# Finer steps, maxima ordered by pairs, a query stack read in halves, and a new order in a three-stage attention kernel

## The chip, the cores and the metric

One core of a Trainium2 chip runs the whole program; the other cores are idle. The time is device microseconds of one execution, and the median of three executions stands for a kernel. The engines are TensorE (PE, with its weight loads PEld), VectorE (DVE), ScalarE (ACT), GpSimd (POOL) and SyncE (SP), which only issues DMAs here.

## The reference

Four batches of x (512 tokens, 128 features) pass three blocks, each on the layer norm of its input, each added to it.

```python
x = x + _L0_attn_ref(_layernorm(x), gamma)          # softmax(-gamma * max(dist_sq, 0)) @ x, 512 x 512
x = x + _L0_xattn_ref(_layernorm(x), ctx, ctx, Wq, bq, Wk, bk, Wv, bv, Wo, bo)
x = x + _L0_ffn_ref(_layernorm(x), router_w, router_b, expert_w, expert_b)
...
dist_sq = sq[:, :, None] + sq[:, None, :] - 2.0 * xy
...
scores = jnp.einsum('bhqd,bhkd->bhqk', q, k) / sqrt(dk)      # 16 heads of 8, 154 keys
scores = scores + slopes[None, :, None, None] * dist[None, None, :, :]
out = einsum('bhqk,bhkd->bhqd', softmax(scores), v)  ... @ Wo.T + bo
...
mask = one_hot(top_k_indices, 8).sum(axis=-2)                # the two best of eight experts
out = einsum('bse,ehd,bsd->bsh', mask, expert_w, hidden_states) + einsum('bse,eh->bsh', mask, expert_b)
```

## The kernel before

The program has five instruction streams. Each is a fixed list of steps, the table `ORDER`: `walk` calls a step `name:b.k` with its batch b and its part k. An engine never leaves its list, so a step that waits on a semaphore holds all that stands behind it. `WARM` says how many matmuls on the constant tile `idle` (results unused) PE issues ahead of a step.

For one batch, with 512 tokens as T = 4 tiles of 128:

- Block 1. `stats1` (DVE) takes mean and variance, `rstd1` (POOL) makes rs and the squared norms `sqp`, `y1` (DVE) normalises. `y1T` (PE, then ACT) transposes y1 and sqp; `dist` makes the four 128x512 distance banks (L913, L914), each reduced on DVE (`rm`, L687) and copied by ACT's relu (L551); `rowmax` and `soft` (L559) make the softmax rows, `probs` transposes them into pT, `self` (L932) multiplies with y1, `gather` (L704, L710, L660, L663) makes x1 and its statistics. There are two distance banks, so tile t waits for the relu of t-2.
- Block 2. `rstd2` makes rs and then x1b = x1 + bo (L521); `y2` (L670), `y2T`, `query` (L945) make q. q is cut into three bf16 parts on ACT and DVE (L757, L759, L761); the last part is there when `q_lo` is counted. SP writes the parts to `q_scratch` and reads them back as `qs`, a stack of 8 head pairs; the key stacks are `kA` (for maxima) and `kB` (for scores). `maxima` (L973, DVE L768) fills a PSUM bank with three query-tile-by-head products of 154 keys and reduces it to negated row maxima `nm`: 64 of them in 22 banks a batch, in two buffers, and two banks are a step. `mcat` cuts nm in three parts, `mT` transposes it, SP carries it through `m_scratch` into six rows of qs. Only then can `scores` (L999 for four banks with the keys over 128, L1003 for sixteen heads; two banks, two items a step) multiply with kB, and ACT's exponential (L611) follows each. `values` (L1019 for the tail keys, L1023) accumulates two halves, `divide` normalises, `aoT` and `wo` (L1050) make x2.
- Block 3. `rstd3`, `y3`, `y3T`, `route` (L1061 and DVE L820 to L835), `mask`, then for each expert `spread` (L1083), `select` (DVE L848) and `experts` (L1096), with `fT` and `store` at the end. Spread uses the banks of the maxima. The last batch does blocks from `divide` on in two halves of 256 tokens.

SP's list holds the DMAs: a load that waits there holds those behind it.

## Time and profile before

| | us |
|---|---|
| median of 3 runs (243.68 to 246.44) | 244.0 |
| the profiled execution | 244.3 |
| its span | 242.5 |
| PE busy, 1206 matmuls | 206.0 (85%) |
| PE weight loads | 104.7 (43%) |
| DVE busy | 157.9 (65%) |
| ACT busy | 109.2 (45%) |
| POOL busy | 36.7 (15%) |
| mean granted clock of PE | 0.972 of full |

The span is cut by the profile into 40 slices, and PE's clock is full in all but two places, at 70 to 80 us and at about 196 us. The chain of work that ended last is PE for 50%, DVE 24%, ACT 9%. In a timeline, neighbouring rows of one engine may overlap a little, since a matmul's row holds its way through the array too: when matmuls follow each other, the distance of their starts is the price of one.

### The profile page before, as it was taken

What the parts mean: (1) busy time and instruction counts of PE and PEld (TensorE: products, weight loads), DVE (VectorE), ACT (ScalarE), POOL (GpSimd) and SP (SyncE); (2) the same over time, 40 slices, a digit from 0 to 9 for tenths busy, and PEclk for the clock granted to TensorE, in tenths of its full rate; (3) what the DMA queues carried; (4) which work ended last, traced back from release to release, by engine and by line L of the source; (5) the groups of instructions that cost most, each with busy time, mean ns of one, the idle gap of its engine ahead of it and who ended that gap; (6) DMA issues with size and microseconds to landing.
All of it is one profiled execution on the core that took longest, in us unless ns stands there. A gap on an engine that the chain in (4) does not pass through costs nothing.

```text
span 242.5 us, 3528 instructions
## 1 busy us (share of the span) xinstructions
PE 206.0 (85%) x1206; PEld 104.7 (43%) x1224; DVE 157.9 (65%) x433; ACT 109.2 (45%) x206; POOL 36.7 (15%) x98
## 2 busy tenths in 40 slices
PE   7488956878958898998999999889987878899994
PEld 2247622436612234474353457643333342335573
DVE  2476536499662488847686699776589513479772
ACT  2286053730317476828635566276133137821300
POOL 5604184300130030005000000130000001002000
PEclk9999999999975999999999999999999979999999
DMA  6997504900204500120152021203601010000011
GB/s 170 310 265 259 110 1 158 223 4 0 57 0 144 119 1 0 41 59 0 68 142 53 0 45 43 58 3 131 130 0 40 11 51 0 0 4 0 1 46 43
DMA packets 23031, 16.91 MB, mean 70 GB/s; under 512 B 10548, under 2 KB 21644, under 8 KB 22924
## 3 DMA queue, kind: packets, MB, share of 16 engines
q1 hardware_dynamic: 23012, 16.67, 26.8%
q8 instruction: 10, 0.16, 0.3%
q14 instruction: 9, 0.07, 0.1%
HBM read 11.29 MB, written 5.37 MB: 69 GB/s over the span
## 4 chain that ended last, share of the span: by engine, by line
PE 50%; DVE 24%; ACT 9%; issue 7%; POOL 4%; DMA 3%; another core or an unknown queue 1%; SPq 0%; ACTq 0%; DVEq 0%; POOLq 0%
DVE nm L768 12%; PE bank L1096 11%; PE bank L875 6%; PE bank L932 5%; PE bank L1023 4%; PE bank L913 4%; PE bank L973 3%; PE bank L1083 3%; DVE y L670 3%; PE bank L1003 3%; POOL rs L459 3%; PE bank L1019 2%; PE bank L870 2%; ACT w L551 2%; DVE x L710 2%
## 5 line engine op out<-in xcount | busy, mean ns | idle before, releaser
L768 DVE TENSOR_REDUCE nm<-bank 128x3 f32<-128x462 f32 x88 | 49.4, 618 | 10.9 <-PE bank L973 10.7
L611 ACT ACTIVATE pt<-bank 128x512 f32<-128x512 f32 x64 | 34.7, 597 | 22.9 <-PE bank L1003 15.2
L973 PE MATMUL bank<-kA,qs 128*128 128x308 bf16 (+1 forms) x172 | 29.2, 264 | 6.5 <-DVE nm L768 5.3
L1096 PE MATMUL bank<-ym,ewT 128*128 128x512 f32 (+1 forms) x80 | 32.5, 511 | 0.3 <-DVE ym L848 0.3
L848 DVE TENSOR_TENSOR ym<-bank,y3T 128x512 f32<-128x512 f32 (+1 forms) x40 | 22.1, 579 | 8.2 <-PE bank L1083 6.8
L870 PE MATMUL bank<-idle 128*128 128x512 bf16 x82 | 22.9, 406 | 3.3 <-DVE idle L655 1.5
L457 POOL TENSOR_SCALAR ve<-mv 128x4 f32<-128x4 f32 (+1 forms) x13 | 2.6, 198 | 151.4 <-DVE mv L663 151.1
L973 PEld LDWEIGHTS bank<-kA,qs 128*128 128x128 bf16 x172 | 12.1, 97 | 28.5 <-DVE nm L768 24.0
L1003 PE MATMUL bank<-qs,kB 128*128 128x512 bf16 x59 | 20.5, 397 | 3.4 <-ACT ptail L611 1.2
L913 PE MATMUL bank<-y1Tg,y1T 128*128 128x512 f32 x32 | 17.9, 641 | 5.5 <-ACT w L551 4.4
L551 ACT ACTIVATE w<-bank,snsq,sgn 128x512 f32<-128x512 f32 x16 | 12.3, 773 | 16.0 <-DVE rm L687 16.0
L687 DVE TENSOR_REDUCE rm<-bank 128x1 f32<-128x512 f32 x16 | 10.9, 688 | 12.6 <-PE bank L914 12.6
L1023 PE MATMUL bank<-pt,vm 128*32 128x512 f32 x128 | 16.9, 598 | 0.3 <-issue 0.3
L670 DVE TENSOR_SCALAR y<-x,mv,rs 128x128 f32<-128x128 f32 x32 | 11.3, 425 | 8.1 <-POOL rs L459 8.0
L1096 PEld LDWEIGHTS bank<-ym,ewT 128*128 128x128 f32 x80 | 13.6, 190 | 5.1 <-DVE ym L848 1.8
L932 PE MATMUL bank<-y,pT 128*128 128x128 f32 x128 | 15.3, 278 | 0.2 <-ACT pT L535 0.2
L870 PEld LDWEIGHTS bank<-idle 128*128 128x128 bf16 x91 | 8.9, 102 | 14.8 <-issue 2.4
L932 PEld LDWEIGHTS bank<-y,pT 128*128 128x128 f32 x128 | 14.6, 192 | 0.6 <-ACT pT L535 0.4
L875 PE MATMUL bank<-ident,y 128*128 128x128 f32 x48 | 7.7, 280 | 6.9 <-DVE y L670 6.9
L559 ACT ACTIVATE w<-w,nrb,sgn 128x512 f32<-128x512 f32 x16 | 12.9, 811 | 1.0 <-DVE nrb L700 0.6
L459 POOL TENSOR_TENSOR rs<-ve,minus_half 128x4 f32<-128x4 f32 (+1 forms) x13 | 13.2, 1012 | 1.1
L1003 PEld LDWEIGHTS bank<-qs,kB 128*128 128x128 bf16 x64 | 6.2, 101 | 14.1 <-ACT pt L611 7.4
(130 smaller groups left out, 275.3 us busy)
## 6 DMA issues: line engine op xcount, KB each, us to landing
qs<-q_scratch SPq DMA_DIRECT2D x8, 384.0 KB, 4.9
q_scratch<-qpart SPq DMA_DIRECT2D x4, 384.0 KB, 2.4
xs<-in_x_dram SPq DMA_DIRECT2D x4, 256.0 KB, 7.2
vm<-in_vm_ones_dram SPq DMA_DIRECT2D x1, 1024.0 KB, 12.0
q_scratch<-qpart SPq DMA_DIRECT2D x4, 256.0 KB, 2.1
kA<-k_scratch SPq DMA_DIRECT2D x8, 120.0 KB, 2.7
kB<-k_scratch SPq DMA_DIRECT2D x8, 120.0 KB, 2.6
out_dram<-ob SPq DMA_DIRECT2D x3, 256.0 KB, 2.4
```

The lines of the kernel that those rows point to most:

```text
L459: g.tensor_tensor(rs[:, at], ve[:, at], minus_half[:, at], ALU.pow).then_inc(rstd[i], 1)
L611: nc.scalar.activation(dst, ST[n % 2][:, :], ACT.Exp).then_inc(exps, 1)
L768: v.tensor_reduce(negated[:, GROUP * g:GROUP * g + heads], MX[n % 2][:, 0:heads * J].rearrange("p (s j) -> p s j", s=heads), AX.X, ALU.max ...
L848: v.tensor_tensor(ym[:, e, at], MX[n % 2][:, at], y3T[:, at], ALU.mult).then_inc(mx_free, 1)
L870: mm(bank_[:, :], idle[:, 0:P], idle[:, :], start=True, stop=True)
L875: last = nc.tensor.transpose(bank_[:, tile(t)], src(t), id_[:, :])
L913: mm((A0S, A1S)[t % 2][b][:, :], y1T[:, tile(t)], y1Tg[:, :], start=True, stop=False)
L932: last = mm(A0S[b][:, tile(t)], pT[:, b % 2, t, u, :], y1[:, b % 2, u, :], start=(u == 0), stop=(u == T - 1))
L973: last = mm(MX[n % 2][:, at * J:(at + heads) * J], qs[:, b % 2, a, tile(t)], kA[:, s:s + heads, a, 0:J], start=True, stop=True)
L1003: last = mm(ST[n % 2][:, :], kB[:, h % 2, h // 2, 0:JM], qs[:, b % 2, h // 2, :], start=True, stop=True)
L1023: last = mm(YV[32 * g:32 * g + 32, :], vm[:, b, R * g + k, :], pt[:, (G * k + g) % PT_RING, :], start=False, stop=(k % 2 == 1), skip_group ...
L1096: last = mm(YMS[b][p][:, at], ewT[:, e, :], ym[:, e, at], start=False, stop=(e == E - 1))
```

## The change

Steps become smaller and the tables that order them are new.

- A scores step is one bank (`PARTS`), a maxima step is one bank (`MAX_GROUPS`), dist is one tile in every batch, self is one tile; `sqT`, `tails` (the products with the tail keys), `invert` (the reciprocal of the softmax sums) and `residual` (x1b) are cut out of larger steps. `residual` has a wait for `q_lo` in front, so x1b is made after the query parts of its batch.
- The maxima run over head pairs first and tiles second: `pieces` and the layout of `nm` change, and the number and width of products in a bank stay.
- The read of qs is four loads in place of two, first pairs 0 to 3, then 4 to 7, with a semaphore each. Maxima wait for the first half at bank 0 and for the second at bank 10.
- `WARM` holds 61 matmuls in place of 91.
- SP has `mT:2` before `store:0`. On POOL, `rstd3:0` comes before `rstd2:2`.

```diff
--- before.py
+++ after.py
@@ ORDER, two of its rows @@
-        y1T:0 dist:0 keys:0 probs:0.0 probs:0.1 probs:0.2 probs:0.3 self:0 y1T:1 y2T:0 query:0 dist:1 probs:1.0
+        y1T:0 sqT:0 dist:0.0 dist:0.1 dist:0.2 dist:0.3 keys:0 probs:0.0 probs:0.1 y1T:1 probs:0.2 sqT:1
...
@@ WARM @@
-    "y1T:0": 14, "probs:0": 1, "y1T:1": 9, "y2T:0": 9, "query:0": 2, "probs:1": 16, "maxima:0": 1, "y2T:1": 16,
-    "query:1": 2, "scores:0": 1, "scores:1": 2, "y2T:2": 3, "wo:1.0": 1, "y3T:1.0": 2, "scores:2": 2, "y2T:3": 2,
-    "query:3": 1, "maxima:3": 1, "divide:2.1": 3, "spread:3.0": 3,
+    "y1T:0": 16, "probs:0": 1, "probs:1": 16, "maxima:0": 2, "y2T:1": 4, "scores:1": 8, "y3T:1.0": 4, "y2T:3": 3,
+    "divide:2.1": 2, "scores:3": 3, "mask:3": 2,
 }
...
@@ -221,7 +246,7 @@
         qf = sb("qf", [P, S])
         qr = sb("qr", [P, S])
         qpart = sb("qpart", [P, 3, S], BF16)
-        nm = sb("nm", [P, T, H])
+        nm = sb("nm", [P, PAIRS, T, 2])
         nmr = sb("nmr", [P, T, H])
         mcat = sb("mcat", [P, T, 3, H], BF16)
         mT = sb("mT", [3 * H, S], BF16)
@@ -269,7 +294,7 @@
         gamma_ready, bqs_ready = sem("gamma_ready"), sem("bqs_ready")
         setup_ps, setup_sb = sem("setup_ps"), sem("setup_sb")
         k_ready, v_ready = sem("k_ready"), sem("v_ready")
-        kA_in, kB_in, qs_in, m_in = sem("kA_in"), sem("kB_in"), sem("qs_in"), sem("m_in")
+        kA_in, kB_in, qs_in, m_in = sem("kA_in"), sem("kB_in"), [sem(f"qs_in{i}") for i in range(2)], sem("m_in")
         stored = [sem(f"stored{i}") for i in range(2)]
         stats = [sem(f"stats{i}") for i in range(3)]
         rstd = [sem(f"rstd{i}") for i in range(3)]
@@ -312,7 +337,7 @@
 
         GROUP = S // J
         GROUPS = -(-T * H // GROUP)
-        MAX_GROUPS = [range(g, min(g + 2, GROUPS)) for g in range(0, GROUPS, 2)]
+        MAX_GROUPS = [range(g, g + 1) for g in range(GROUPS)]
         ITEMS = R * G + G
 
         def maxima_fill(b, g):
@@ -333,7 +358,7 @@
         def rowmax_count(b, t):
             return t + 1 if b == 0 else T + b
 
-        PARTS = [(i, i + 1) for i in range(0, ITEMS, 2)]
+        PARTS = [(i,) for i in range(ITEMS)]
 
         RUNS = ((0, 3), (3, 2), (5, 1))
         ONE = 16
@@ -403,8 +428,11 @@
                     sp.wait_ge(st_ps, (b - 1) * ITEMS)
                 sp.wait_ge(q_out, 3 * ONE * (b + 1))
                 for s in range(2):
-                    load(qs[s * ROWS:(s + 1) * ROWS, b % 2, :, :],
-                         q_scratch.rearrange("(a s c) k n -> s (c k) a n", s=2, c=DK)[s], qs_in)
+                    load(qs[s * ROWS:(s + 1) * ROWS, b % 2, 0:PAIRS // 2, :],
+                         q_scratch.rearrange("(a s c) k n -> s (c k) a n", s=2, c=DK)[s, :, 0:PAIRS // 2], qs_in[0])
+                for s in range(2):
+                    load(qs[s * ROWS:(s + 1) * ROWS, b % 2, PAIRS // 2:PAIRS, :],
+                         q_scratch.rearrange("(a s c) k n -> s (c k) a n", s=2, c=DK)[s, :, PAIRS // 2:PAIRS], qs_in[1])
 
             def divide(b, f):
                 if f == 0 and b + 1 < B:
@@ -513,6 +541,9 @@
 
             def rstd2(b, _):
                 norm(1, b, mv2, ve2, rs2)
+
+            def residual(b, _):
+                pool.wait_ge(q_lo, b + 1)
                 if b == 0:
                     pool.wait_ge(weights_in, W_LOADS * ONE)
                 if b >= 2:
@@ -524,7 +555,7 @@
             def rstd3(b, p):
                 norm(2, b, mv3, ve3, rs3, p, tiles(b, p))
 
...
 
         @block.scalar
         def _(act):
@@ -540,11 +571,13 @@
                 act.wait_ge(y1T_ps, b + 1)
                 copy(y1T[:, :], A0S[b][:, :]).then_inc(y1T_sb, 1)
                 nc.scalar.activation(y1Tg[:, :], A0S[b][:, :], ACT.Copy, scale=gam2[:, :]).then_inc(y1T_sb, 1)
+
+            def sqT_(b, _):
                 act.wait_ge(sqT_ps, b + 1)
                 copy(sqT[:, :], col16(A1S[b])[:, 0:S]).then_inc(y1T_sb, 1)
 
             def dist(b, k):
-                for t in (range(k, k + 1) if b == 0 else range(T)):
+                for t in range(k, k + 1):
                     act.wait_ge(rm_ready, T * b + t + 1)
                     if b >= 2:
                         act.wait_ge(pT_ps, T * (b - 2) + t + 1)
@@ -644,7 +677,7 @@
                 at = span(b, p)
                 copy(fT[:, at], YMS[b][p][:, at]).then_inc(fT_sb, 1)
 
...
 
@@ -682,7 +715,7 @@
                 normalise(0, b, lambda t: xs[:, b, t, :], mv1, rs1, y1[:, b % 2])
 
             def dist(b, k):
-                for t in (range(k, k + 1) if b == 0 else range(T)):
+                for t in range(k, k + 1):
                     dve.wait_ge(dist_ps, T * b + t + 1)
                     v.tensor_reduce(rm[:, t:t + 1], (A0S, A1S)[t % 2][b][:, :], AX.X, ALU.max).then_inc(rm_ready, 1)
 
@@ -699,9 +732,11 @@
                 settle()
                 v.tensor_scalar(nrb[:, b % 2, cols], rma[:, cols], 0.0, nsgn[:, :], ALU.max, ALU.mult).then_inc(rowmax, 1)
 
-            def gather(b, _):
+            def invert(b, _):
                 dve.wait_ge(p_ready, T * (b + 1))
                 done(v.reciprocal(rd1[:, :], den[:, b % 2, :]))
+
+            def gather(b, _):
                 settle()
                 dve.wait_ge(self_ps, b + 1)
                 if b >= 1:
@@ -761,7 +796,7 @@
                 v.tensor_tensor(qpart[:, 2, :], qr[:, :], qpart[:, 1, :], ALU.subtract).then_inc(q_lo, 1)
 
             def maxima(b, k):
-                negated = nm[:, :, :].rearrange("p t h -> p (t h)")
+                negated = nm[:, :, :, :].rearrange("p a t s -> p (a t s)")
                 for g in MAX_GROUPS[k]:
                     n, heads = maxima_fill(b, g), min(GROUP, T * H - GROUP * g)
                     dve.wait_ge(mx_full, n + 1)
@@ -771,7 +806,7 @@
 
             def mcat_(b, _):
 
-                neg = nm[:, :, :].rearrange("p t (a s) -> p t s a", s=2)
+                neg = nm[:, :, :, :].rearrange("p a t s -> p t s a")
                 rest = nmr[:, :, :].rearrange("p t (s a) -> p t s a", s=2)
                 part = [mcat[:, :, i, :].rearrange("p t (s a) -> p t s a", s=2) for i in range(3)]
                 dve.wait_ge(mx_free, maxima_fill(b, GROUPS))
@@ -856,7 +891,7 @@
                                 x2[:, b % 2, at], ALU.add).then_inc(out_ready, 1)
 
...
 
         @block.tensor
@@ -900,14 +935,16 @@
                     pe.wait_ge(consts, 5)
                 pe.wait_ge(normed[0], b + 1)
                 turn(A0S[b], lambda t: y1[:, b % 2, t, :]).then_inc(y1T_ps, 1)
+
+            def sqT_(b, _):
                 pe.wait_ge(sq_ready, b + 1)
                 turn(col16(A1S[b]), lambda t: sqp[:, t, :], ident16).then_inc(sqT_ps, 1)
 
-            def dist(b, _):
+            def dist(b, k):
 
 
                 pe.wait_ge(y1T_sb, 3 * (b + 1))
-                for t in range(T):
+                for t in range(k, k + 1):
                     if t >= 2:
                         pe.wait_ge(w_relu, T * b + t - 1)
                     mm((A0S, A1S)[t % 2][b][:, :], y1T[:, tile(t)], y1Tg[:, :], start=True, stop=False)
@@ -923,14 +960,13 @@
                 pe.wait_ge(p_ready, T * b + t + 1)
                 turn((A0S, A1S)[t % 2][b], lambda u: w[:, b % 2, t, tile(u)]).then_inc(pT_ps, 1)
 
-            def self_(b, _):
-                pe.wait_ge(pT_sb, T * b + 3)
-                for t in range(T):
-                    if t == T - 1:
-                        pe.wait_ge(pT_sb, T * (b + 1))
-                    for u in range(T):
-                        last = mm(A0S[b][:, tile(t)], pT[:, b % 2, t, u, :], y1[:, b % 2, u, :], start=(u == 0), stop=(u == T - 1))
-                last.then_inc(self_ps, 1)
+            def self_(b, t):
+                pe.wait_ge(pT_sb, T * b + max(t, 2) + 1)
+                for u in range(T):
+                    last = mm(A0S[b][:, tile(t)], pT[:, b % 2, t, u, :], y1[:, b % 2, u, :], start=(u == 0),
+                              stop=(u == T - 1))
+                if t == T - 1:
+                    last.then_inc(self_ps, 1)
 
             def y2T_(b, _):
                 pe.wait_ge(pT_sb, T * (b + 1))
@@ -950,7 +986,7 @@
                 found, n = [], GROUP * g
                 while n < min(GROUP * (g + 1), T * H):
                     heads = 2 if n % 2 == 0 and n + 2 <= min(GROUP * (g + 1), T * H) else 1
-                    found.append((n // H, n % H // 2, n % 2, heads))
+                    found.append((n // 2 % T, n // (2 * T), n % 2, heads))
                     n += heads
                 return found
 
@@ -963,8 +999,10 @@
                         pe.wait_ge(mx_free, maxima_fill(b, 0))
                     warm(MX[maxima_fill(b, 0) % 2], f"maxima:{b}")
                     pe.wait_ge(kA_in, 2 * ONE * (b + 1))
-                    pe.wait_ge(qs_in, 2 * ONE * (b + 1))
+                    pe.wait_ge(qs_in[0], 2 * ONE * (b + 1))
                 for g in MAX_GROUPS[k]:
+                    if GROUP * g <= H * T // 2 < GROUP * (g + 1):
+                        pe.wait_ge(qs_in[1], 2 * ONE * (b + 1))
                     n = maxima_fill(b, g)
                     if n >= 2:
                         pe.wait_ge(mx_free, n - 1)
@@ -1004,20 +1042,21 @@
                                   qs[:, b % 2, h // 2, :], start=True, stop=True)
                     last.then_inc(st_ps, 1)
 
+            def tails(b, f):
+
+                if f == 0 and b == 0:
+                    pe.wait_ge(v_ready, 2 * B + R)
+                if f == 0 and b >= 1:
+                    pe.wait_ge(x2_ready, b)
+                if f == 1:
+                    pe.wait_ge(pvs_sb, 2 * b + len(YMS[b]))
+                warm(YV, f"tails:{b}.{f}")
+                pe.wait_ge(exps, b * ITEMS + G)
+                for g in range(G):
+                    mm(YV[32 * g:32 * g + 32, :], vt[:, b, g, f, :], ptail[:, g, :],
+                       start=True, stop=False, skip_group_check=True)
+
             def values(b, k):
-
-                if k == 0 and b == 0:
-                    pe.wait_ge(v_ready, 2 * B + R)
-                if k == 0 and b >= 1:
-                    pe.wait_ge(x2_ready, b)
-                if k == 2:
-                    pe.wait_ge(pvs_sb, 2 * b + len(YMS[b]))
-                if k % 2 == 0:
-                    warm(YV, f"values:{b}.{k}")
-                    pe.wait_ge(exps, b * ITEMS + G)
-                    for g in range(G):
-                        mm(YV[32 * g:32 * g + 32, :], vt[:, b, g, k // 2, :], ptail[:, g, :],
-                           start=True, stop=False, skip_group_check=True)
                 pe.wait_ge(exps, b * ITEMS + G * (k + 2))
                 for g in range(G):
                     last = mm(YV[32 * g:32 * g + 32, :], vm[:, b, R * g + k, :], pt[:, (G * k + g) % PT_RING, :],
@@ -1101,9 +1140,9 @@
                 pe.wait_ge(fT_sb, b + p + 1)
                 turn(YMS[b][p], lambda t: fT[:, tile(t)], rows=rows_of(b, p)).then_inc(fT_ps, 1)
 
...
```

On PE, the place between the query of batch 0 and the first maxima (y is the normalised batch, w the softmax rows, pT their transposes, kA and qs the stacks). Before:

```order
L945 MATMUL bank<-y2T,wT 128x512
L913 MATMUL bank<-y1Tg,y1T 128x512
L914 MATMUL bank<-sqT,ones 128x512
...
L870 MATMUL bank<-idle 128x512 x16
L875 MATMUL bank<-ident,w 128x128 x4
L870 MATMUL bank<-idle 128x512
L973 MATMUL bank<-kA,qs 128x308
```

Now:

```order
L950 MATMUL bank<-y1Tg,y1T 128x512
L951 MATMUL bank<-sqT,ones 128x512
L981 MATMUL bank<-y2T,wT 128x512
L905 MATMUL bank<-idle 128x512 x16
L910 MATMUL bank<-ident,w 128x128 x16
L966 MATMUL bank<-y,pT 128x128 x16
L905 MATMUL bank<-idle 128x512 x2
L1011 MATMUL bank<-kA,qs 128x308
```

The distances of batch 1 stand before the query product, and all its softmax transposes and its self products (L966) before the first maxima; before, only one of four transposes stood there.

On PE, from the last maxima of batch 0 to the scores and the next maxima. Before:

```order
L932 MATMUL bank<-y,pT 128x128 x16
L875 MATMUL bank<-ident,mcat 48x128 x4
L870 MATMUL bank<-idle 128x512 x16
L875 MATMUL bank<-ident,y 128x128 x4
L870 MATMUL bank<-idle 128x512 x2
L945 MATMUL bank<-y2T,wT 128x512
L870 MATMUL bank<-idle 128x512
L999 MATMUL bank<-qs,kB 32x512 x16
L1003 MATMUL bank<-qs,kB 128x512 x4
L913 MATMUL bank<-y1Tg,y1T 128x512
```

Now:

```order
L905 MATMUL bank<-idle 128x512 x4
L910 MATMUL bank<-ident,y 128x128 x4
L910 MATMUL bank<-ident,mcat 48x128 x4
L981 MATMUL bank<-y2T,wT 128x512
L950 MATMUL bank<-y1Tg,y1T 128x512
L951 MATMUL bank<-sqT,ones 128x512
L950 MATMUL bank<-y1Tg,y1T 128x512
L951 MATMUL bank<-sqT,ones 128x512
L1037 MATMUL bank<-qs,kB 32x512 x16
L1041 MATMUL bank<-qs,kB 128x512 x2
L1056 MATMUL bank<-ptail,vt 32x512 x4
```

The self products and twelve idle matmuls are gone from here, and two distances of batch 2 stand ahead of the scores; its other two lie among the maxima.

On DVE, after the maxima of batch 1 (x and st are x1 or x2 and their statistics, lg the router's logits). Before:

```order
L784 TENSOR_TENSOR mcat<-nmr,mcat 128x4x16
L670 TENSOR_SCALAR y<-xs,mv,rs 128x128 x4
L791 RECIPROCAL rd<-bank 128x32
L793 TENSOR_TENSOR ao<-bank,rd 128x4x64
L704 RECIPROCAL rd<-den 128x4
L710 SCALAR_TENSOR_TENSOR x<-bank,rd,xs 128x128 x4
L660 BN_STATS st<-x 128x6 x4
L663 BN_AGGR mv<-st 128x2 x4
L801 TENSOR_TENSOR x<-bank,x1b 128x512
```

Now:

```order
L819 TENSOR_TENSOR mcat<-nmr,mcat 128x4x16
L836 TENSOR_TENSOR x<-bank,x1b 128x512
L693 BN_STATS st<-x 128x6 x4
L696 BN_AGGR mv<-st 128x2 x4
L737 RECIPROCAL rd<-den 128x4
L745 SCALAR_TENSOR_TENSOR x<-bank,rd,xs 128x128 x4
L693 BN_STATS st<-x 128x6 x4
L696 BN_AGGR mv<-st 128x2 x4
L703 TENSOR_SCALAR y<-x,mv,rs 128x128 x8
L703 TENSOR_SCALAR y<-xs,mv,rs 128x128 x4
```

x2 of batch 0 (L836) is made before x1 of batch 2 (L745), the division of batch 0 lies among the maxima, and y1 of batch 3 has gone behind y3 and y2.

## Rows read from the trace of the kernel before

**Rows 1.** PE by stretches: start and end, length, busy (matmuls), clock, DMA share, GB/s

```profile
108.00:131.50 23.50, 21.25 (x114) 1.00 0.27 68
...
sum 242.50, PE 206.01; mean PE 14.71
```

**Rows 2.** The same stretches, matmuls on the tile idle (L870) alone

```profile
sum 242.50, PE 22.85; mean PE 1.63
```

**Rows 3.** Timeline of PE: start, us, line, tiles; starts of maxima (L973) and scores

```profile
47.20 0.56 PE L973 MATMUL bank<-kA,qs 128*128 128x308 bf16 x4
...
73.45 1.04 PE L999 MATMUL bank<-qs,kB 128*32 128x512 bf16 x8
...
86.11 0.57 PE L973 MATMUL bank<-kA,qs 128*128 128x308 bf16 x4
...
108.07 0.61 PE L999 MATMUL bank<-qs,kB 128*32 128x512 bf16 x8 [0.32 <-issue]
...
131.51 0.56 PE L973 MATMUL bank<-kA,qs 128*128 128x308 bf16 x4
...
156.56 0.61 PE L999 MATMUL bank<-qs,kB 128*32 128x512 bf16 x8 [0.19 <-issue]
...
175.94 0.56 PE L973 MATMUL bank<-kA,qs 128*128 128x308 bf16 x4
...
196.18 1.04 PE L999 MATMUL bank<-qs,kB 128*32 128x512 bf16 x8 [1.07 <-DMA qs<-m_scratch]
```

**Rows 4.** Timeline of DVE: row maximum, y, q_lo (L761), selects, banks of maxima

```profile
11.98 0.69 DVE L687 TENSOR_REDUCE rm<-bank 128x1 f32<-128x512 f32 x1 [1.18 <-PE bank L914]
...
22.91 1.11 DVE L670 TENSOR_SCALAR y<-xs,mv,rs 128x128 f32<-128x128 f32 x4
...
30.48 2.05 DVE L670 TENSOR_SCALAR y<-x,mv,rs 128x128 f32<-128x128 f32 x4 [1.50 <-POOL rs L459]
...
66.83 1.82 DVE L670 TENSOR_SCALAR y<-x,mv,rs 128x128 f32<-128x128 f32 x4 [1.50 <-POOL rs L459]
...
120.79 0.69 DVE L761 TENSOR_TENSOR qpart<-qr,qpart 128x512 bf16<-128x512 f32 x1
121.58 1.89 DVE L848 TENSOR_TENSOR ym<-bank,y3T 128x512 f32<-128x512 f32 x3
...
179.04 9.85 DVE L768 TENSOR_REDUCE nm<-bank 128x3 f32<-128x462 f32 x18 [0.27 <-PE bank L973]
```

**Rows 5.** Timelines of POOL, PE and ACT: single steps

```profile
11.17 1.03 POOL L459 TENSOR_TENSOR rs<-ve,minus_half 128x4 f32<-128x4 f32 x1
...
22.18 3.84 PE L932 MATMUL bank<-y,pT 128*128 128x128 f32 x32 [0.20 <-ACT pT L535]
...
30.34 1.09 POOL L521 TENSOR_TENSOR x1b<-x,cols 128x512 f32<-128x512 f32 x1
...
68.71 0.66 PE L875 MATMUL bank<-ident,y 128*128 128x128 f32 x4 [2.02 <-DVE y L670]
...
111.23 2.17 ACT L611 ACTIVATE pt<-bank 128x512 f32<-128x512 f32 x4
...
131.90 1.88 PE L1096 MATMUL bank<-ym,ewT 128*128 128x512 f32 x4
```

**Rows 6.** Chain of work that ended last, before the last scores: start, us

```profile
191.24 2.04 DMA m_scratch<-mT
...
193.30 2.54 DMA qs<-m_scratch
```

**Rows 7.** The page's DMA issues: engine, count, KB each, us to landing

```profile
qs<-q_scratch SPq DMA_DIRECT2D x8, 384.0 KB, 4.9
...
kA<-k_scratch SPq DMA_DIRECT2D x8, 120.0 KB, 2.7
```

**Rows 8.** PE in stretches of two microseconds: length, busy, clock, DMA

```profile
70.00:72.00 2.00, 1.95 (x2) 0.50 0.00 0
```

150 lines of the change are left out of this document (88 added, 62 removed).

## Prediction

> **What bounds the kernel now.** I read the busy time by stretches first. PE is busy for 206.0 of 242.5 us, but 22.9 of that are matmuls on the tile `idle`, which compute nothing [rows 1, 2]. So about 59 us (36.5 idle, 22.9 filled) hold no work. Then I read, in PE's timeline, where each batch's maxima (L973) and scores (L999) begin [rows 3]. Call M0 to M3 and S0 to S3 the eight starts: M = 47.2, 86.1, 131.5, 175.9; S = 73.45, 108.1, 156.6, 196.2. The kernel is a chain of rounds from S to S: 34.6, 48.5, 39.6, and 46.3 us from S3 to the end. Each round has three parts, each with its own limit.
>
> From S to the next M: scores, and beside them the chain x1, y2, query, q_lo (L761), scratch, `qs`. Maxima: 22 banks on DVE, 18 of which took 9.85 us, 0.55 each [rows 4]; 12.2 us is their floor. Then the turnaround: the last maximum of batch 3 ends at 188.9, S3 is at 196.2, with two DMAs of 2.04 and 2.54 us in between [rows 3, 4, 6]; 6.8 us where PE is free in time for the transpose. Of M and the turnaround only the work that waits inside can be saved; the rest is order.
>
> **The change part by part.** Matmuls, reductions and exponentials keep their number and shape, so their durations stay, and only places and waits move. I walked the new order row by row, each step beginning at the later of its engine's last step and of what it waits for, with durations from the rows.
>
> *Opening.* y1 of batch 1 now stands on DVE ahead of the first row maximum. Its input rs lands at 12.2, it takes 1.11, so the maximum starts at 13.4 instead of 11.98 [rows 4, 5]. The two row maxima that are now put together delay soft a little more: self of batch 0 starts at 24.0, where it was 22.2 [rows 5]. That is 1.9 us lost. y2 of batch 0 then took 2.05 us [rows 4] while POOL's x1b of 1.09 us ran [rows 5]; the same form without it took 1.11 [rows 4]. `residual` puts x1b behind q_lo, which gives 0.94 back. Distances 1.1 to 1.3 then slip in ahead of query:0, and q_lo comes 1.4 us later than before (40.1). The 16 idle matmuls and the transposes of w cover its way; self:1 now runs before the maxima, 43.3 to 47.0. M0 is 47.4, as before (47.2).
>
> The half read: SP issues four loads of 0.42 us in place of two. Its landing is not in the trace; 120 KB took 2.7 us, 384 KB 4.9 [rows 7], a half of 192 KB lies between, and I take 3.3. First halves are ready at M0 and M1 by it; at 4.9, M0 would be at most 1 us late.
>
> *Batch 1's attention.* Before, self:1 follows the maxima of batch 0, y2 takes 1.82, again with x1b beside it, and ends at 68.65 [rows 4]; PE has idled 2.02 us for it [rows 5]. Now gather:1 (four x1, four statistics, four aggregates: 2.4 us on DVE) lies between banks 14 and 15: 22 banks of 0.56 and 2.4 from the first reduction at 47.8 end at 62.6 (before: 59.9); y2:1 (1.1) and mcat (0.95) follow, to 64.65. With mT's transpose 0.45, its copy 0.6, the DMAs of 2.04 and 2.54 [rows 6] and 0.35 to PE, S0 = 70.6, under which y2T:1, query:1, dist 2.2 and 2.3 fit. **Term 1: -2.8.** What it uncovers: values_in (2.4) and query:1 wait on DVE for each other; q_lo:1 is 71.0, was 75.4, and M1 needs it only by 76.
>
> *Round 0.* Before M1 PE had the four distances of batch 2, with their waits for ACT's relu (78.3 to 84.3, 6 us). They are ahead of S0 now. Exponentials go at 0.54 each [rows 5]; eight of them and one soft (0.8) put values:0.0 at S+6.4 and M1 at S+7.3 (was 12.7). The maxima: 12.2, two divides 1.6, and 1.5 of banks held behind a score that waits for soft: 15.3 (15.1). Turnaround 6.8. 29.4 against 34.6: **term 2: -5.2.**
>
> *Round 1.* Before, x1 of batch 2 waits behind the whole self:2, wo:0 behind aoT, y3:0 behind x1b on POOL, and q_lo ends at 121.5, 13.4 after S1 [rows 4]. Now PE has wo:0 done at S-4.6; x2 and its statistics (1.9) end at S-2.6; self:2 ends at S-2.9 and gather:2 (2.4) at S-0.1. POOL makes rs in 1.3 each, y3:0 ends at S+1.2, y2:2 at S+2.7, y1:3 at S+3.8. y2T and query ride between the scores: y3T:0 at S+2.3, route:0 on PE S+3.9 to 4.8, on DVE to 7.5; qf and its copy end at 7.65, q_lo 1.8 later, S+9.45. Then eight selects of 0.63 [rows 4] and two distance maxima of 0.7 on DVE, with PE's spreads, first expert products and distances behind each: M2 = S+17.3 (23.4). The maxima take over two distances and six expert products of 0.86 [rows 5]; PE bounds that part, 19.6 (18.3). Turnaround 6.8. 43.7 against 48.5: **term 3: -4.8.**
>
> *Round 2.* y3:1 and y2:3 are a little earlier (y2:3 at S+3.7, was 4.6, since x1b again leaves it), M3 = S+16.3 (19.4), with five expert products moved beside the maxima, where PE waits for DVE anyway: 12.7 (13.0). Turnaround 7.0, since values:2.2 delays the transpose. 36.0 against 39.6: **term 4: -3.6.** *Last round.* All scores are out by S+13.5 (17), two values products and a tails step leave the stretch after spread 2.0; wo:2 and y3:2 come later, hidden under scores. PE would gain 2.6, DVE (eight selects, three divides, two wo) gives about 1.5 of it: **term 5: -1.5.**
>
> The rest: sqT, tails and invert as steps of their own cost nothing, they lie under the waits above. POOL's rstd1:2 is behind residual:0 now and is done at 42.7, y1:2 at 43.8, before M0. SP's order (mT:2 before store:0) takes two issues from a DMA on the path, 0.
>
> Sum of the terms: -17.9. A walk in which every step starts on the instant is too kind; I give back 1 us a round, 4 in all, chosen, not measured. 242.5 - 17.9 + 4 = 228.6. The profiled execution was 244.3, 1.8 over its span, and 0.3 over the median of 244.0: 228.6 + 1.8 - 0.3 = 230.1; I say 230.
>
> **Two rules beside the rows.** The first bears on where x1b goes. The rows: y2 lost 0.94 of x1b's 1.09 [rows 4, 5]. In its new place in rounds 1 and 2 x1b lies beside selects, which read PSUM and one SBUF tile; no row shows the two together. Bound: 0 to 0.94 a batch, taken as 0, since the slowed y2 is of another form. The Trainium skill, "SBUF — State Buffer", Terms, has the port pair of DVE and GpSimd locked for a whole instruction, and the contending DVE operations are those in a two-port mode or with two SBUF inputs. By that rule the new place is free and the sum stands; without it, it is up to 1.9 worse. The second is the clock, in rival D.
>
> **The rivals.** A, the walk holds with 2 to 6 us given back: 225 to 234.
>
> B, half of it: PE takes its steps strictly in order, and with one-product steps more steps have a semaphore wait of their own. For it: in L973's groups PE already idles behind DVE's banks and in S0 to M1 behind ACT. Against: ACT is busy 45% only, and the longest gaps (turnaround of batch 0, S1 to M2) are of dependence, not of handing over. Half of 17.9: 244 - 9 = 235, up to 239.
>
> C, only the opening and the two uncontended y2: the finer steps change no round because PE was the bound in them. In 108.0 to 131.5 PE is busy 21.25 of 23.5 us [rows 1]. Against: that busy time counts the tail of each waiting matmul; at issue prices (0.22 a score, 0.88 a values step, 0.86 an expert, 1.07 a distance, 0.2 a bank, 0.44 four transposes) round 1 holds 39 us of its 48.5. It gives 244 - 2.8 = 241, within 2%.
>
> D, slower: the change takes 30 of 91 idle matmuls out. In the trace the clock fell once for ten microseconds, after PE had idled 2.02 us up to 68.71 [rows 5]: at 70 to 72 it is 0.50, 1.2 GHz, and two matmuls of query took 1.95 us of it [rows 8]. y2T:1 loses 12 of its 16 idle matmuls, and y2T:0 and y1T:1 all 18. If the clock stays down, a packed PE loses half of each such microsecond; 28 us at 1.2 GHz beyond the 13 of before eat the whole gain of 14, 38 make it slower by 2% (250). Against: the new order puts self, distances and transposes where the idle ones were; the longest gap that my walk leaves is 2.4 us, before S3, and 1.7 before dist 2.3. The Trainium skill, "TensorE: Matmul & The Clock Gate", "What's actually happening", has the slow state as the default and activity as what lifts it, which speaks against taking filler out; by it alone D would be as likely as the gaps are long, and this trace agrees in that the fall follows a gap, though other gaps of two microseconds (before 32.6, before 40.2) had none.
>
> **How the numbers follow.** A 0.63, B 0.20, C 0.12, D 0.05. A measurement here tells about 2% from no change, so faster means under 239.1 and slower over 248.9: faster 0.83 (A and B), same 0.12, slower 0.05. The range goes down to 224 (nothing given back and a clock that stays up in S0 to M1: 226.1, and 2 of that stretch's slow clock) and up to 238, where most of B is in and C and D (0.17) are out. A's own range is 225 to 234.
>
> **What would show it.** S0 near 70.6 and self of batch 0 near 24.0; y2 of batches 0, 1 and 3 at 1.1 us; M1 about 7 after S0, S1 near 101; M2 17 to 18 after S1; turnarounds still 6.8 to 7.3; the last round 45. Term 1 is wrong if S0 stays at 73; terms 2 and 3 if PE waits for single exponentials between maxima banks; D is right if the clock is 0.50 in more than the 13 us. The prediction is wrong as a whole if the maxima parts grow by what the parts before them lose.

## The result and the profile after

The changed kernel took 230.3 us in the median (228.8 to 232.4 in four executions), the kernel before beside it 243.8 (241.3 to 246.4): a ratio of 0.946, 95% interval 0.931 to 0.961. It is faster by 13.5 us; the forecast was 230, 224 to 238. The profiled execution was the longest of the four, 232.4 us with a span of 230.6.

From the page of the kernel after: the span, busy time by engine, and the granted clock in 40 slices.

```profile
span 230.6 us, 3497 instructions
...
PE 197.7 (86%) x1178; PEld 101.4 (44%) x1194; DVE 156.1 (68%) x433; ACT 108.8 (47%) x206; POOL 34.8 (15%) x98
...
PEclk9997997999999999999999999999999999999999
...
L905 PE MATMUL bank<-idle 128*128 128x512 bf16 x54 | 15.9, 437 | 1.9 <-DVE idle L688 1.5
...
qs<-q_scratch SPq DMA_DIRECT2D x16, 192.0 KB, 3.6
```

PE holds 181.8 us of work (197.7 less 15.9 on `idle`), where it held 183.2 [rows 1, 2]; so 10.5 of the 11.9 us of span are less waiting (48.8 us instead of 59.3), and only 1.4 are shorter work.

The timeline of PE after: the starts of the maxima (L1011) and of the scores (L1037).

```profile
49.10 0.36 PE L1011 MATMUL bank<-kA,qs 128*128 128x308 bf16 x2
...
71.56 0.61 PE L1037 MATMUL bank<-qs,kB 128*32 128x512 bf16 x8
...
79.11 0.37 PE L1011 MATMUL bank<-kA,qs 128*128 128x308 bf16 x2
...
101.58 0.61 PE L1037 MATMUL bank<-qs,kB 128*32 128x512 bf16 x8 [0.56 <-issue]
...
119.64 0.56 PE L1011 MATMUL bank<-kA,qs 128*128 128x308 bf16 x4
...
146.43 0.61 PE L1037 MATMUL bank<-qs,kB 128*32 128x512 bf16 x8 [0.47 <-DMA qs<-m_scratch]
...
164.08 0.56 PE L1011 MATMUL bank<-kA,qs 128*128 128x308 bf16 x4 [0.74 <-DMA qs<-q_scratch]
...
185.68 0.61 PE L1037 MATMUL bank<-qs,kB 128*32 128x512 bf16 x8 [2.19 <-issue]
```

Against [rows 3]: S0 at 71.6 (73.45), and the rounds 30.0, 44.9, 39.3 and 44.9 us (34.6, 48.5, 39.6, 46.3). Ten of the twelve microseconds of span were gained before S2 (1.9 up to S0, 4.6 and 3.6 in the first two rounds); the third round gave 0.4 where 3.6 were forecast.

### The profile page after: what moved, and what is told of

The parts are those of the page before. It is cut to its first block, busy times and chain, and to the rows that moved or that the text cites. A ratio compares the mean times of both kernels' runs of the same rounds, so it can differ in the third digit from the quotient of the medians.

```text
span 230.6 us, 3497 instructions
## 1 busy us (share of the span) xinstructions
PE 197.7 (86%) x1178; PEld 101.4 (44%) x1194; DVE 156.1 (68%) x433; ACT 108.8 (47%) x206; POOL 34.8 (15%) x98
## 4 chain that ended last, share of the span: by engine, by line
PE 53%; DVE 21%; ACT 9%; DMA 6%; issue 6%; POOL 3%; SPq 0%; DVEq 0%; ACTq 0%; POOLq 0%
PE bank L1135 11%; DVE nm L803 11%; PE bank L910 7%; PE bank L1062 6%; PE bank L1011 4%; PE bank L966 4%; PE bank L950 4%; PE bank L1041 4%; PE bank L1122 2%; ACT w L592 2%; PE bank L1056 2%; PE bank L1089 2%; ACT ptail L644 2%; DMA q_scratch<-qpart 2%; DVE rm L720 2%
## 5 line engine op out<-in xcount | busy, mean ns | idle before, releaser
L803 DVE TENSOR_REDUCE nm<-bank 128x3 f32<-128x462 f32 x88 | 50.0, 620 | 14.1 <-PE bank L1011 13.8
L644 ACT ACTIVATE pt<-bank 128x512 f32<-128x512 f32 x64 | 35.8, 598 | 20.3 <-PE bank L1041 15.5
L1011 PE MATMUL bank<-kA,qs 128*128 128x308 bf16 (+1 forms) x172 | 29.5, 263 | 7.0 <-DVE nm L803 5.5
L1011 PEld LDWEIGHTS bank<-kA,qs 128*128 128x128 bf16 x172 | 12.8, 97 | 31.9 <-DVE nm L803 22.2
L950 PE MATMUL bank<-y1Tg,y1T 128*128 128x512 f32 x32 | 18.5, 663 | 6.6 <-ACT w L584 5.8
L905 PE MATMUL bank<-idle 128*128 128x512 bf16 x54 | 15.9, 437 | 1.9 <-DVE idle L688 1.5
L966 PE MATMUL bank<-y,pT 128*128 128x128 f32 x128 | 16.1, 279 | 0.0
L966 PEld LDWEIGHTS bank<-y,pT 128*128 128x128 f32 x128 | 15.0, 192 | 0.5 <-ACT pT L566 0.3
L644 ACT ACTIVATE ptail<-bank 128x512 f32<-128x512 f32 x16 | 8.7, 598 | 10.0 <-PE bank L1037 10.0
L703 DVE TENSOR_SCALAR y<-x,mv,rs 128x128 f32<-128x128 f32 x32 | 9.8, 377 | 5.2 <-POOL rs L487 5.2
L487 POOL TENSOR_TENSOR rs<-ve,minus_half 128x4 f32<-128x4 f32 (+1 forms) x13 | 12.6, 971 | 1.1
L1122 PE MATMUL bank<-maskT,spread 128*128 128x512 bf16 (+1 forms) x38 | 11.1, 336 | 1.3 <-ACT maskT L566 0.7
L1041 PEld LDWEIGHTS bank<-qs,kB 128*128 128x128 bf16 x64 | 5.9, 99 | 12.7 <-ACT pt L644 8.5
## 6 DMA issues: line engine op xcount, KB each, us to landing
vm<-in_vm_ones_dram SPq DMA_DIRECT2D x1, 1024.0 KB, 12.7
```

The source lines that it names most:

```text
L644: nc.scalar.activation(dst, ST[n % 2][:, :], ACT.Exp).then_inc(exps, 1)
L803: v.tensor_reduce(negated[:, GROUP * g:GROUP * g + heads], MX[n % 2][:, 0:heads * J].rearrange("p (s j) -> p s j", s=heads), AX.X, ALU.max ...
L905: mm(bank_[:, :], idle[:, 0:P], idle[:, :], start=True, stop=True)
L950: mm((A0S, A1S)[t % 2][b][:, :], y1T[:, tile(t)], y1Tg[:, :], start=True, stop=False)
L966: last = mm(A0S[b][:, tile(t)], pT[:, b % 2, t, u, :], y1[:, b % 2, u, :], start=(u == 0), stop=(u == T - 1))
L1011: last = mm(MX[n % 2][:, at * J:(at + heads) * J], qs[:, b % 2, a, tile(t)], kA[:, s:s + heads, a, 0:J], start=True, stop=True)
```

## The experiments

All ratios are to the kernel before on the same chip (another chip for the last series: y1 moved, all together, both orders put back). The yardstick is the changed kernel run again in the first series: 229.75 us, ratio 0.943 (0.938 to 0.947). "+4 us" below means a quotient of two such ratios times 229.75, good to about 1.5 us.

**The yardstick.**

> The changed kernel once more, as the yardstick of this series (nothing in it is altered). Every theory expects a ratio of 0.94 to 0.95 to the kernel before, 228 to 232 us. The walk theory (the gain is a sum of shorter waits in the opening and the rounds) expects, in an execution of 227 us, the score stages to start near 71.5, 101, 146 and 184 us, the one stretch that was long in the first profile (from the third to the fourth score stage, 39.25 us) coming down toward 37, because the write of the third query part of batch 3 took 4.1 us to land there and 1.7 in the other batches.

Its executions of 228.9 to 232.8 us differed by the mean clock that PE was granted: 228.9 us at 1.000, 229.3 to 230.1 at 0.993, 232.5 at 0.985, 232.8 at 0.978. In its trace each fall is a stretch of three to four microseconds at 0.5, three before the last microseconds (31 to 35, 55 to 58, 185 to 188 us). The profile of the first run has two (17 to 20, 34 to 37). So the clock of one kernel falls in different places from one execution to the next. Three falls go with 3.9 us more than none, 1.3 us a fall; the executions with one (0.993) are 0.4 to 1.2 us longer. This ties time to clock by their going together. The third round stayed long, 39.2: that cause is not chance.

**x1b back behind the second rstd.**

```diff
-            def residual(b, _):
-                pool.wait_ge(q_lo, b + 1)
```

> x1b's sum is made right behind the second rstd again, as in the kernel before; all else is the changed kernel. Contention theory: the second normalisation of each batch meets it and goes from 1.11 to about 1.8 to 2.05 us, once per batch on the path (opening and three rounds), and the third normalisation of batch 2 falls from 1.80 to 1.11. Sum: four times 0.7 to 0.9, less 0.7, so +2.1 to +2.9 us, ratio to the changed kernel 1.009 to 1.013. Rival, the normalisations lie beside other work: 0 to +0.5 us.

233.4 us, ratio 0.960 (0.956 to 0.965): +4.3 us. The sizes in the trace are the forecast's for batches 0, 2 and 3 (y2 takes 2.05, 1.80, 1.80), while batch 1 was free at 1.11, since its x1b ran at 59.8, beside the maxima. That is 2.2 us, less the 0.7 of y3:2: 1.5 by this reckoning, and the time is above the forecast of 2.1 to 2.9. The rest may go with the clock: its mean over the executions was 0.977, the yardstick's 0.990. The two profiled executions, both at 0.978, differ by 0.55 us only (233.37 and 232.82), so neither share is measured by itself.

**x1b moved, nothing else,** in the kernel before.

```diff
+            def residual(b, _):
+                pool.wait_ge(q_lo, b + 1)
```

> The kernel before with one part of the change alone: x1b's sum leaves the place behind the second rstd and waits for the third query part. Contention theory: the second normalisation goes from 2.05, 1.82 (batches 0, 1 to 3) to about 1.1 us in each batch; 0.94 comes off the opening, about 0.7 off each of two to three rounds, so -0.9 (opening alone) to -2.9 us, ratio 0.988 to 0.996 to the kernel before. Rival, x1b in its new place meets another two-input operation of VectorE and gives it back: 0.

240.2 us, ratio 0.981 (0.976 to 0.985): -4.8 us, above the forecast range. From its timelines of DVE, POOL and PE:

```profile
32.67 1.26 DVE L673 TENSOR_SCALAR y<-x,mv,rs 128x128 f32<-128x128 f32 x4 [1.50 <-POOL rs L459]
...
68.19 1.11 DVE L673 TENSOR_SCALAR y<-x,mv,rs 128x128 f32<-128x128 f32 x4 [1.50 <-POOL rs L459]
...
199.01 1.09 POOL L524 TENSOR_TENSOR x1b<-x,cols 128x512 f32<-128x512 f32 x1
...
199.15 1.04 DVE L673 TENSOR_SCALAR y<-x,mv,rs 128x128 f32<-128x128 f32 x1 [1.48 <-POOL rs L459]
...
69.36 0.66 PE L878 MATMUL bank<-ident,y 128*128 128x128 f32 x4 [1.32 <-DVE y L673]
...
72.92 0.62 PE L1002 MATMUL bank<-qs,kB 128*32 128x512 bf16 x8
```

y2 of batch 0 is 1.26 instead of 2.05 and y2 of batch 1 is 1.11 instead of 1.82, PE waits 1.32 us for it instead of 2.02 [rows 5], and then the clock does not fall: the ten microseconds at 0.5 from 69 to 79 us, seen before the change [rows 8], are gone, and round 0 is 33.0 instead of 34.6. From the transpose of y2 to S0 it is 3.6 us instead of 4.7. So the contention itself cost 0.7 us and the fall behind it some 2.8. That the fall hangs on this one wait is read from one trace of each kernel. Two falls are in the trace, at 9 to 16 us (new) and at 193 to 197 (where the kernel before has one at 196 to 199). The fourth row shows the new clash too: one tile of y3 took 1.04 instead of 0.34 beside x1b.

**The query stack read whole.**

```diff
-                    load(qs[..., 0:PAIRS // 2, :], ..., qs_in[0])
-                    load(qs[..., PAIRS // 2:PAIRS, :], ..., qs_in[1])
+                    load(qs[s * ROWS:(s + 1) * ROWS, b % 2, :, :], ..., qs_in[0])
```

> The query stack is read in two whole loads of 384 KB again, with one count for both; the order of the maxima stays pair by pair. By the walk only two of the four batches wait for the stack: the first maxima of batch 0 come 1.3 to 1.5 us later (4.9 us to land against 3.5), those of batch 3 likewise 0 to 1.4; in batches 1 and 2 the stack has landed by either way before the score products of the tails are through. Sum +1.3 to +2.9 us, ratio 1.006 to 1.013. Rival, the half read is worth its 1.4 us in all four batches: +5.6 us. Rival, it is hidden in all: 0.

237.0 us, ratio 0.973 (0.968 to 0.978): +7.4 us, three times the forecast. PE's timeline at the maxima of batch 3, first of the whole read, then of the yardstick:

```profile
166.07 0.56 PE L1006 MATMUL bank<-kA,qs 128*128 128x308 bf16 x4 [2.70 <-DMA qs<-q_scratch]
```

```profile
163.17 0.56 PE L1011 MATMUL bank<-kA,qs 128*128 128x308 bf16 x4 [0.44 <-DMA qs<-q_scratch]
```

The places are nearly as expected: M0 comes at 48.9 instead of 47.5, M1 0.4 us later behind S0, M2 unchanged, M3 2.3 later behind S2: 4.1 us. The two profiled executions, with equal clocks of 0.977 and 0.978, differ by 2.4 us all the same, because a fall at 55 to 58 us stretched the yardstick's maxima of batch 0 (16.0 instead of 14.7) and hid the loss at M0. The executions without a profile had a mean clock of 0.975 (0.993 in the yardstick), which at 1.3 us a fall is some 3 us more. So 4.1 us are seen in the trace, and the rest is put down to the clock without a run that shows it.

**Steps of two.** Each odd score product and each odd bank of maxima stands right behind its even one.

```diff
-        scores:0.4 scores:0.5 tails:0.0 scores:0.6 probs:2.0 scores:0.7
+        scores:0.4 scores:0.5 tails:0.0 scores:0.6 scores:0.7 probs:2.0
```

> The same work and the same order, but score products and banks of maxima taken two at a time again on TensorE, ScalarE and VectorE (each odd one moved right behind its even one). Theory of the moved stages (what pays is x2, the first sum, the next batch's attention coming earlier beside the work that covers them): most of the gain stays, +1 to +4 us to the changed kernel. Rival, the fineness itself pays (each walk alternates between two engines' queues and a step of two blocks the other one): the mixed stretches of the three rounds lose 3 to 4 us each, +9 to +12 us.

235.1 us, ratio 0.961 (0.955 to 0.967): +4.5 us. S0 is 72.5, the rounds 31.1, 46.1, 38.9, 44.9; beside the yardstick 1.3 us each in the opening and rounds 0 and 1, nothing after: 2.4 us between the two profiled executions, both at a mean clock of 0.978. The time is just above the forecast of 1 to 4 us. A third of the gain is gone without the alternation, and 0.961 stays with all the rest of the change. The steps themselves are still of one bank, each with its wait, so the price of such waits was not tested.

**Batch 1's attention put back.**

```diff
-        ... probs:1.3 self:1.0 self:1.1 self:1.2 self:1.3 maxima:0.0 ... y2T:1 mT:0 query:1
+        ... probs:1.3 maxima:0.0 ... maxima:0.21 self:1.0 self:1.1 self:1.2 self:1.3 mT:0 y2T:1 query:1
```

(on DVE gather:1 and y2:1 behind mcat:0)

> The changed kernel with one move of the change taken back: batch 1's self sum on TensorE and its first sum on VectorE stand behind batch 0's maxima again (the split of the maxima into parts ahead of the second normalisation), all else the changed kernel. By the walk: the second normalisation of batch 1 ends near 69 instead of 64.9 us, the query product that stands ahead of the first scores on TensorE waits for it, so the first score stage starts 2 to 3 us later (near 74, as before the change 73.45) and TensorE stands idle for some 3 us there, which lets the clock fall: +3 to +6 us, ratio 0.955 to 0.967 to the kernel before. Rival, the first scores wait for the maxima's parts anyway, which now come 1.1 us earlier: -1 to +1 us.

241.8 us, ratio 0.992 (0.988 to 0.997): +12.1 us. Timelines of PE and DVE:

```profile
68.40 0.40 PE L910 MATMUL bank<-ident,mcat 128*48 128x128 bf16 x4
...
73.68 0.66 PE L910 MATMUL bank<-ident,y 128*128 128x128 f32 x4 [3.91 <-DVE y L703]
75.12 2.04 PE L981 MATMUL bank<-y2T,wT 128*128 128x512 f32 x2 [0.78 <-ACT y2T L566]
76.95 1.92 PE L950 MATMUL bank<-y1Tg,y1T 128*128 128x512 f32 x2
...
81.48 0.61 PE L1037 MATMUL bank<-qs,kB 128*32 128x512 bf16 x8
...
68.56 1.13 DVE L745 SCALAR_TENSOR_TENSOR x<-bank,rd,xs 128x128 f32<-128x128 f32 x4 [2.19 <-PE bank L966]
...
72.51 1.12 DVE L703 TENSOR_SCALAR y<-x,mv,rs 128x128 f32<-128x128 f32 x4 [1.50 <-POOL rs L487]
```

Self (3.8), x1 and its statistics (2.4), rs (1.5), y2, its transpose and copy, the query product and two distances now lie one behind another between PE's last product of the maxima and the first score: 16.6 us where the yardstick has 8.2. I had forgotten that dist 2.2 and 2.3 stand between query:1 and scores:0 and that mT waits for self. The clock falls behind the wait of 3.91, so the query product takes 2.04 instead of 1.10. And self:1 no longer covers the way of the query stack: PE waits 2.08 us for it up to M0 (47.5), and the clock falls there too, from 47 to 54 us, amid the maxima (17.8 us instead of 16.0). The forecast had 3 to 6 us. Rounds 0 to 3 stay as they are (29.8, 45.1, 39.3, 45.9).

**The order at S1 put back.**

```diff
-        maxima:1.19 self:2.0 maxima:1.20 aoT:0 maxima:1.21 self:2.1 probs:2.3 mT:1 wo:0 self:2.2 self:2.3 scores:1.0
+        maxima:1.19 maxima:1.20 maxima:1.21 probs:2.3 mT:1 self:2.0 self:2.1 self:2.2 self:2.3 aoT:0 scores:1.0 scores:1.1 wo:0
```

(DVE: gather:2 ahead of wo:0, y2:2 ahead of y3:0; POOL alike)

> The changed kernel with the order of the second turnaround taken back: TensorE takes batch 2's self sum and batch 0's attention output behind the transposed maxima of batch 1 and one score product pair ahead of wo, VectorE takes batch 2's first sum ahead of x2, and the second normalisation ahead of the third, as in the kernel before. By the walk: x2 and with it routing, the third normalisation and the selection of batch 0's experts come 2.5 to 4 us later, and the stretch from the second score stage to the third maxima grows from 18.06 to 20.5 to 22 us; the maxima themselves stay at 19.3. Forecast +2.5 to +4 us, ratio 0.953 to 0.960 to the kernel before. Rival, what counts in that stretch is only the number of operations of VectorE, whatever their order: 0 to +0.5 us.

239.6 us, ratio 0.976 (0.971 to 0.982): +8.1 us. The forecast was 2.5 to 4 us. The profiled execution took 244.4 us, 4.7 above the median, so the rows show the chain and their sizes are on the high side:

```profile
97.39 5.46 PE L966 MATMUL bank<-y,pT 128*128 128x128 f32 x32
102.69 0.60 PE L910 MATMUL bank<-ident,ao 128*128 128x128 f32 x4
103.34 1.67 PE L905 MATMUL bank<-idle 128*128 128x512 bf16 x7
104.95 0.62 PE L1037 MATMUL bank<-qs,kB 128*32 128x512 bf16 x8
...
111.36 0.91 PE L910 MATMUL bank<-ident,y 128*128 128x128 f32 x4 [3.28 <-DVE y L703]
```

The whole self sum of batch 2 now delays S1 itself (turnaround 9.0 instead of 6.7), x2 is done at S1+2.4 instead of S1-3.4, and PE stands for 3.3 us, behind which the clock falls again (111.6 to 118.5 us). It had also fallen within the self sum (98.0 to 101.4). From S1 to M2 it is 24.95, in the kernel before 23.4 [rows 3], in the yardstick 18.1.

**Fetched instructions.** The slow third round. In the trace of the kernel after, the third query part of batch 3 and the maxima of batch 3 are slow to land. SyncE's timeline (each second row waits for the write ahead of it), then from the DMA view the landing of the third part (154 to 162 us) and the packet at 156 to 157:

```profile
154.22 2.25 SPq L371 DMA_DIRECT2D q_scratch<-qpart  x3
160.27 1.78 SPq L371 DMA_DIRECT2D qs<-q_scratch  x4
...
180.08 0.32 SPq L371 DMA_DIRECT2D m_scratch<-mT  x1
182.85 0.26 SPq L371 DMA_DIRECT2D qs<-m_scratch  x1
```

```profile
q_scratch<-qpart SPq DMA_DIRECT2D x1, 128.0 KB, 4.1
...
q8 instruction: 1, 0.02, 11.6%
```

6.05 us from the first issue to the read, in batch 2 only 3.67 (109.41 to 113.08). One packet of the queue q8 lies at 156 us and is busy for 11.6% of 16 engines times 1 us, 1.9 us on one engine; another lies at 180. The queue has nine packets in the run. The theory is that the third part waits for the engine that carries it. Test: 26 tiny products at the start of PE, which moves the packets if they are PE's program.

```diff
+                    for _ in range(26):
+                        mm(A0[:, 0:8], idle[:, 0:P], idle[:, 0:8], start=True, stop=True)
```

> The changed kernel with 26 products of eight columns more on TensorE, in the 1.35 us in which it waits for the first normalisation anyway; they do nothing but put some 52 instructions ahead of all that follow. In the profiles a packet of the instruction queue q8 of about 16 KB, some every 20 us, stands at 156 us beside the write of the third query part of batch 3 (4.1 us to land against 1.7) and at 180 beside the write of the maxima of batch 3 (2.8 us until read back against 1.6). Fetch theory: these are TensorE's own instructions, they take place at fixed positions of its program, and 52 instructions more move each 3 to 4 us earlier: that write lands in 1.7 to 2.3 us, that of the maxima in 1.6, and rounds 2 and 3 are 1 to 3 us shorter (span of the profiled execution), unless a moved packet falls on another write. Rival, the slow landings have another cause (the positions in the transfer order, the store of an earlier batch): 4.1 and 2.8 stay and the time is that of the changed kernel, 0 to +0.5 us.

The same views of this kernel (the share of the packet is now over two microseconds, 150 to 152, so 4.0% are 1.3 us on one engine):

```profile
153.03 2.25 SPq L371 DMA_DIRECT2D q_scratch<-qpart  x3
157.19 1.78 SPq L371 DMA_DIRECT2D qs<-q_scratch  x4
...
178.09 0.32 SPq L371 DMA_DIRECT2D m_scratch<-mT  x1
179.69 0.26 SPq L371 DMA_DIRECT2D qs<-m_scratch  x1
```

```profile
q_scratch<-qpart SPq DMA_DIRECT2D x1, 128.0 KB, 2.2
...
q8 instruction: 1, 0.02, 4.0%
```

The packets, ten now, moved to 151 and 175 us, the landings fell to 2.2 us and to 1.6 until read back (2.8 before), and the third round to 37.2 us: M3 comes 16.8 after S2 instead of 17.65, the turnaround is 6.5 instead of 7.8. Another packet now fell on batch 2 (111 us; its read 5.65 us behind the first issue), where nothing waits (M2 stays at S1+18.1). The other profiles agree. From the first issue to the read it is 5.5 to 6.1 us at batch 3 in all eight in which nothing was put ahead in PE's program, and 4.2 us in the four in which idle or tiny products stand there (this one, the three with filled holes below). In the run that moves y1:1 on DVE alone the packets stay at S2+10 and S2+34, as here before. So the fetch theory holds for the trace. In time it is 229.6 us, ratio 0.938 (0.933 to 0.942), 1.2 us below the yardstick, within what the runs can't tell apart.

**Idle products in the two holes of the opening.**

```diff
+    "dist:0.2": 7, "dist:1.2": 8,
...
+                    warm(MX[1], f"dist:{b}.{t}")
```

> The changed kernel with 15 idle products more on TensorE, 7 in the hole before the third distance tile of batch 0 (2.0 us, waiting for w) and 8 in the one before the third of batch 1 (1.9 us), into a free bank. Clock theory: the granted clock was 0.5 for 3 to 4 us behind one or both of these holes in each profile (17 to 20 and 34 to 37 us in one, 31 to 35 in another); with the holes filled it stays 1.0 until 49 us, the first maxima come at 46 to 47 instead of 47.5 to 49.1, and the time falls by 1 to 2 us, ratio 0.935 to 0.940 to the kernel before. Rival, the clock is low there beside a path that runs over ScalarE and VectorE: 0. Rival, the clock merely falls later: 0.

228.7 us, ratio 0.935 (0.931 to 0.939): -1.8 us, at the edge of what is told apart. PE's timeline and stretches after the change:

```profile
15.13 1.10 PE L950 MATMUL bank<-y1Tg,y1T 128*128 128x512 f32 x2 [1.98 <-ACT w L584]
16.06 0.38 PE L951 MATMUL bank<-sqT,ones 128*128 128x512 bf16 x1
16.80 1.78 PE L950 MATMUL bank<-y1Tg,y1T 128*128 128x512 f32 x2 [0.36 <-ACT w L584]
```

```profile
16.00:18.00 2.00, 1.64 (x4) 0.77 1.09 311
18.00:20.00 2.00, 2.00 (x5) 0.50 1.06 373
```

and with the hole filled:

```profile
12.91 1.67 PE L905 MATMUL bank<-idle 128*128 128x512 bf16 x7
14.94 1.13 PE L951 MATMUL bank<-y1Tg,y1T 128*128 128x512 f32 x2 [0.36 <-ACT w L584]
...
16.70 1.10 PE L951 MATMUL bank<-y1Tg,y1T 128*128 128x512 f32 x2 [0.41 <-ACT w L584]
```

The distance takes 1.10 instead of 1.78, M0 is 46.4 instead of 49.1 (47.5 in the yardstick), and the clock is 1.0 until 225 us. The mean clock of five of its six executions was 0.991 or more. Of the eight profiles of the changed order that have the first hole at 1.96 to 1.98 us, five show a fall within two microseconds behind it; of the four in which it is filled or smaller, none does.

**Idle products in more places:** besides the two holes, one behind each bank of batch 0 and 12 instead of 3 ahead of the last scores.

```diff
+    "bank:0": 1, "scores:3": 12,
...
+                    if b == 0:
+                        warm(ST[1], "bank:0")
```

> The two holes of the opening filled with 7 and 8 idle products, one idle product more behind each of batch 0's 22 banks of maxima, and 12 instead of 3 ahead of the last batch's scores, where TensorE stood for 2.2 to 2.5 us. Clock theory: the falls seen at 55 to 58 and 185 to 188 us in a second profile of the changed kernel go too, the granted clock is 1.0 nearly throughout, executions agree within 1 us at 227 to 228 us, ratio 0.930 to 0.937 to the kernel before. Rival, the products cost what they give: 22 times 0.2 us behind the banks delays VectorE's maxima by up to 4 us, or those ahead of the scores delay them by up to 1 us: 229 to 234 us.

229.0 us, ratio 0.936 (0.931 to 0.940). The clock is 1.0 to 227 us, and nothing is gained over the two holes: the rounds read 30.1, 45.1, 38.1, 44.9, with the two holes alone 29.8, 44.9, 38.0, 44.9. One of its six executions took 265.5 us at a mean clock of 0.753; no other run here has one like it, and its cause is open. So idle products did not always hold the clock up.

**Batch 1's normalisation behind the third row maximum.**

```diff
-        stats1:0 y1:0 stats1:1 y1:1 dist:0.0 rowmax:0.0 dist:0.1 rowmax:0.1 weights:0 dist:0.2 dist:0.3
+        stats1:0 y1:0 stats1:1 dist:0.0 rowmax:0.0 dist:0.1 rowmax:0.1 weights:0 dist:0.2 y1:1 dist:0.3
```

> The changed kernel with batch 1's first normalisation moved on VectorE from ahead of batch 0's first row maximum to behind the third, where VectorE stood idle for 1.7 us; TensorE transposes it only at 23 us. By the walk its 1.11 us was what made batch 0's row maxima, exponentials and self sum late: the self sum of batch 0 starts at 23.9 instead of 25.0, the first maxima and the first scores 1.0 to 1.1 us earlier, the hole before the third distance tile shrinks from 2.0 to 0.9 us, so that the clock has one reason less to fall. Forecast -1.0 to -2.0 us, ratio 0.935 to 0.939 to the kernel before. Rival, the opening is set by the keys' products and copies, which follow the same products on TensorE but not the row maxima: 0.

228.9 us, ratio 0.937 (0.931 to 0.942): -1.5 us, not told apart by itself. In the trace M0 is 45.1 and S0 67.6, 2.4 and 3.6 us before the yardstick's. The third distance is at 13.61 with a wait of 0.61 instead of 1.98, and no fall comes before 183 us. One edit takes away both the 1.1 us and the hole behind which the clock could fall.

**Together.**

> The edits that earlier runs or the profile point to, in one kernel: idle products in the two holes of the opening (4 and 8; alone, 7 and 8 gave a ratio of 0.9352 against 0.9427), batch 1's first normalisation behind the third row maximum (1.1 us by the profile), batch 3's x1b ahead of the third rstd of batch 2, so that it meets no normalisation (the third normalisation of batch 2 took 1.80 instead of 1.11 us), and 16 products of eight columns at the start, which with the idle ones put some 56 instructions ahead, so that no packet of the queue q8 falls on the write of batch 3's maxima (2.44 us until read back with the holes alone, 1.6 free). If the terms add: 1.8, 1.1, 0.7 and 0.8 off 229.75 give 225 to 226 us, ratio 0.918 to 0.925. Rival, they overlap (the opening's two are one, the last two hide beside ScalarE): 227.5 to 228.5 us, as with the holes alone.

226.4 us (225.9 to 227.6), ratio 0.931 (0.927 to 0.935): 2.9 us below the changed kernel, the intervals of the two ratios apart. It beats both kernels. y3:2, from DVE's timeline of the kernel after and of this one:

```profile
192.45 1.80 DVE L703 TENSOR_SCALAR y<-x,mv,rs 128x128 f32<-128x128 f32 x4 [1.48 <-POOL rs L487]
```

```profile
187.98 1.12 DVE L703 TENSOR_SCALAR y<-x,mv,rs 128x128 f32<-128x128 f32 x4 [1.49 <-POOL rs L487]
```

The terms did not add to 225: the two edits of the opening are one, as the rival had it (M0 is 45.3 here and 45.1 with y1:1 moved alone). Both writes of batch 3 are free of packets (4.2 us to the read of the stack, 1.6 until the maxima are read back), and round 2 is 37.2. The clock still fell once in the profile, at 53.6 to 57 us. The median lies between the two forecasts.

## Why the prediction was right, and where it was not

**The mechanism.** Right: a sum of shorter waits, with PE's work unchanged. The two moves on which the terms rest were tested one by one, and each undone takes back more than its term (12 and 8 us), x1b and the half read likewise (4 and 7). The four add to far more than the 13.5 that they brought together. So none can be read as a share: the rest of the order is tuned to each, and a wait that reappears can have a fall of the clock behind it. Terms 2, 4 and 5 had no run of their own; they rest on the rounds of the profile.

**The opening** (forecast S0 70.6, self:0 24.0, M0 47.4). In the first profile 71.6, 25.0, 49.1; in the yardstick's 71.2, 23.5, 47.5. Where the clock stayed up until self:0, the walk was right to half a microsecond. The loss by y1:1, forecast at 1.9 with the row maxima put together, is real; moved, self:0 is at 22.5. y2 of batch 0 took 1.26, not 1.11, so x1b's going gave 0.8 back, not 0.94. What the step missed is that it opened a hole on PE (1.98 us) which the clock could fall behind.

**Half read** (3.3 us taken): 3.6 on the page (median of 16). M0, M1 and M2 did not wait for it. M3 waited 0.74 us, because the write ahead of it was late; with the packets moved that write was on time, and M3 did not wait.

**Round 0** (29.4): 30.0. M1 came 7.55 after S0 (7.3), the maxima 15.8 (15.3), the turnaround 6.7 (6.8). But the term named the order alone. The kernel before had the clock at half for the first 6.5 us of this round, and with x1b moved and that fall absent its round is 33.0. So some 1.6 of the 4.6 us gained go with the clock, which no term of the sum counted, and about 3 with the order, where 5.2 were forecast: that the round came out near the forecast is in part luck.

**Round 1** (43.7): 44.9; M2 18.1 after S1 (17.3), the maxima 19.7 (19.6), the turnaround 7.1. q_lo ended at S+9.7 (9.45), y2:2 at S+3.1 (2.7), route:0 at S+7.5 (7.5). The row by row walk held to 0.4 us up to q_lo; then the selects and the last distance maximum waited 2.2 us in sum for PE's products, 1.8 of them for the spreads.

**Round 2** (36.0): 39.3, the term that failed. M3 came 17.65 after S2 (16.3), the maxima 13.85 (12.7), the turnaround 7.8 (7.0). The step "M3 = S+16.3" let q_lo's write land as in the other batches; it took 2.4 us longer to the read, 1.9 of them behind an instruction packet (4.16 without it), and the turnaround has the second. Without both the round is 37.2: M3 at S+16.8, the turnaround 6.5. What stays wrong in the term is the maxima, 13.85 in either trace; they were to fall by 0.3 from 13.0 beside the five expert products and grew by 0.9. No run tells why.

**Last round** (44.8): 44.9. Right, though y3:2 paid 0.7 us that was not in the list: x1b of batch 3 waits on POOL behind rstd3:2 and so starts at 192.31, 0.14 before that y3. The claim that x1b is free beside the selects held: 111.38 to 112.47 on POOL, and the two selects at 111.44 took 1.29, as the two at 114.86 did without it. The Trainium skill, "SBUF — State Buffer", Who interferes with whom, says that an instruction of VectorE with at most one input in SBUF, outside the two-port modes, does not contend with GpSimd; the trace agrees for these selects, 1.29 us with x1b and without.

**The allowance** of 4 us, 1 a round, was the chosen number: the walk without it gives 224.6, the profiled span was 230.6, so 6.0 were needed. Of these 2.0 are the two packets in round 2, 1.2 the rest of that round, and 1.0 the opening; 0.6 and 1.15 are in rounds 0 and 1. The median execution needed 4.0, just what was given back. That the time is 230.3 beside a forecast of 230 is luck: the profile has two late writes and two falls of the clock that the sum lacks, and it lacks the long fall of before, which the sum did not count as a gain.

**Rival D.** Wrong as a whole: the clock stood at half for 6.8 us in the profile, before the change for 13.7. But its mechanism moved the results: 20 of the 32 falls in the fourteen profiles (the last three microseconds left out) begin during a wait of PE of 1.9 us or more or within 2.2 us behind it. In both orders put back such falls stand in the trace; for x1b and the whole read only the mean clock points to them. **Rival B** named one-product steps as a loss. Their alternation is worth up to 4.5 us; what their extra waits cost was not tested. **Rival C** is out: rounds 0 and 1 became 4.6 and 3.6 us shorter.

## What to carry to other kernels

Walk the new order row by row from durations of the old trace; it held to about a microsecond per stage here, the third round apart, which was 3.3 us off. Allow slack where a DMA is on the path. Where two products of one engine stand in a hole of another, price a wait with the fall of the clock that may follow it (about 1.3 us a fall here), and look for an operation that can leave a hole's beginning, before filling it with idle products. Undoing one part of a tuned order tells that it matters, not how much it brought.

## What the runs showed of the hardware

- The granted clock fell to half in stretches of mostly three to four microseconds (26 of 32 falls; five lasted about 7, one 10), at places that differ between executions of one kernel. Of 34 waits of PE of 1.86 us or more, 20 had a fall (1.98 us up to 15.13, fall from 17; 2.45 us up to 185.03, fall from 185) and 14 had none (2.19 us up to 185.68). Seven falls stand amid batch 0's banks, where PE waits only some 0.2 to 0.3 us for most. Times went with the mean clock: 228.9 us at 1.000, 232.8 at 0.978.
- The DMA engines also carry nine packets of some 16 KB of an instruction queue (q8), which move when TensorE's program grows: 52 more of its instructions at the start moved the two of batch 3 from 156 and 180 to 151 and 175 us. One that lay beside a 128 KB write went with 4.1 us until it landed instead of 2.2 (1.7 in the other batches), one beside the 48 KB write of the maxima with 2.8 us until read back instead of 1.6.
- POOL's sum of 1.09 us costs a normalisation from SBUF that it meets 0.7 to 0.8 us: 1.80 instead of 1.11 for four tiles, 2.05 instead of 1.26 in batch 0, 1.04 instead of 0.34 for one tile. It cost the selects, which read PSUM, nothing (1.29 us for two).
